# Attention with a quantised gate on one core: two rounds of four key tiles a step, and score banks lent to other fills

## The reference

```python
xn = layernorm(x)                                     # (4, 1024, 128)
Q, K, V = ((xn @ W).reshape(4, 1024, 16, 64) for W in (Wq, Wk, Wv))
raw = einsum('bshe,bthe->bsth', Q, K / sqrt(64))
attn = softmax(raw, axis=2)                           # over the 1024 keys t
A = gelu(einsum('bsth,bthe->bshe', attn, V).reshape(4, 1024, 1024))
s = xn + A @ Wpost
xq = quantise(xn), wq = quantise(weight)              # blocks of 32 onto a grid of 6-bit floats, times the block's scale
g = silu(xq @ wq.T + bias)
out = x + s * g
```

## Time and profile before

| | us |
|---|---|
| median of 3 runs | 1503.74 |
| lowest, highest | 1503.32, 1508.24 |
| profiled execution | 1504.28 |
| its span, first to last instruction | 1502.5 |
| TensorE busy | 1456.3 |
| GpSimd busy | 1144.7 |
| VectorE busy | 1080.7 |
| ScalarE busy | 804.7 |

### The profile page before, as it was taken

How to read it: one execution, slowest core, us unless ns; L and a number is a source line. 1 busy time by engine, 2 the same in 40 slices (tenths; PEclk the granted TensorE clock), 3 DMA queues, 4 the chain that set the end, 5 groups by cost and what they waited for, 6 DMA issues and landing times.

```text
span 1502.5 us, 25748 instructions
## 1 busy us (share of the span) xinstructions
PE 1456.3 (97%) x10369; PEld 794.2 (53%) x10369; DVE 1080.7 (72%) x1408; ACT 804.7 (54%) x1123; POOL 1144.7 (76%) x545
## 2 busy tenths in 40 slices
PE   5999999999999999999999999999999999999988
PEld 2555455555555555555555554555555555555478
DVE  6577777777777777777777777777777777777632
ACT  3455564555556565455555655555555555555563
POOL 0778788878887887887888778788778878877930
PEclk9999999999999999999999999999999999999999
DMA  2000000000000000000000000000000000002361
GB/s 76 1 8 15 8 15 29 16 8 15 15 8 15 15 13 24 15 14 8 15 15 15 8 15 14 9 15 15 8 15 8 1 1 1 1 1 80 118 220 49
DMA packets 25589, 35.40 MB, mean 24 GB/s; under 512 B 1792, under 2 KB 15872, under 8 KB 25472
## 3 DMA queue, kind: packets, MB, share of 16 engines
q1 hardware_dynamic: 25472, 33.76, 6.4%
HBM read 19.07 MB, written 14.68 MB: 22 GB/s over the span
## 4 chain that ended last, share of the span: by engine, by line
PE 88%; DVE 10%; issue 1%; ACT 1%; DMA 0%; POOL 0%; SPq 0%; ACTq 0%
PE acc L397 26%; PE scores L384 21%; PE peaks L368 11%; PE extra L287 8%; PE scores L388 7%; DVE half_maxes L807 5%; PE extra L317 4%; PE extra L300 4%; PE scores L456 4%; PE extra L324 2%; PE extra L338 1%; DVE extra L782 1%; DVE extra L783 1%; DVE extra L784 1%; DVE quant L785 1%
## 5 line engine op out<-in xcount | busy, mean ns | idle before, releaser
L696 POOL TENSOR_TENSOR prob_sum<-prob_sum,probs 128x1024 f32<-128x1024 f32 x384 | 912.1, 2375 | 236.7 <-ACT probs L571 209.3
L807 DVE TENSOR_REDUCE half_maxes<-peaks 128x2 f32<-128x1024 f32 x504 | 611.5, 1213 | 282.4 <-PE peaks L368 281.2
L571 ACT ACTIVATE probs<-scores 128x1024 f32<-128x1024 f32 x512 | 497.2, 1023 | 385.3 <-PE scores L388 375.4
L397 PE MATMUL acc<-probs,vals 128*64 128x512 f32 x2048 | 487.9, 597 | 0.0
L397 PEld LDWEIGHTS acc<-probs,vals 128*64 128x64 f32 x2048 | 137.2, 137 | 246.3 <-issue 218.1
L823 DVE RECIPROCAL inv_sum<-inv_sum 128x128 f32<-128x128 f32 x256 | 240.1, 941 | 0.0
L368 PE MATMUL peaks<-k_hi,q_hi 64*128 64x512 f32 x1008 | 226.0, 443 | 0.0
L384 PE MATMUL scores<-q_hi,k_hi 64*128 64x512 f32 x1024 | 202.7, 392 | 0.0
L388 PE MATMUL scores<-max_rows,ones_r 64*128 64x512 f32 x1024 | 202.2, 390 | 0.0
L384 PE MATMUL scores<-q_hi,k_lo 64*128 64x512 f32 x1024 | 202.1, 390 | 0.0
L384 PE MATMUL scores<-q_lo,k_hi 64*128 64x512 f32 x1024 | 202.0, 390 | 0.0
(11 more groups left out here) (147 smaller groups left out, 1025.6 us busy)
## 6 DMA issues: line engine op xcount, KB each, us to landing
att_scratch<-att SPq DMA_DIRECT2D x48, 256.0 KB, 2.0
probs<-att_scratch SPq DMA_DIRECT2D x8, 512.0 KB, 9.1
xTs<-att_scratch SPq DMA_DIRECT2D x4, 512.0 KB, 7.9
out_dram<-xn SPq DMA_DIRECT2D x8, 256.0 KB, 4.1
x_in<-in_L_attn_X SPq DMA_DIRECT2D x3, 512.0 KB, 4.0
q_hi_back<-att_scratch SPq DMA_DIRECT2D x2, 512.0 KB, 4.2
q_lo_back<-att_scratch SPq DMA_DIRECT2D x2, 512.0 KB, 5.0
k_hi_back<-att_scratch SPq DMA_DIRECT2D x2, 512.0 KB, 6.6
```

The lines of the kernel that those rows point to most:

```text
L397: last = mm(acc[own[h], :], vals[(s // 2) % 2][:, j, own[h]], probs[j][:, h, :], start=(j == 0), stop=(j == KT - 1), tile_position=col[h])
L571: sa.activation(probs[j][:, :, :], scores[j % 2][:, :, :], ACT.Exp, scale=DH ** -0.5).then_inc(probs_ready, 1)
L696: gp.tensor_tensor(prob_sum[s % 2][:, :, :], before[:, :, :], probs[j][:, :, :], ALU.add).then_inc(probs_summed, 1)
L807: v.tensor_reduce(half_maxes[:, :, f // 2, f % 2], peaks[:, :, :], AX.X, ALU.max).then_inc(peaks_read, 1)
```

## The change

A step now has two rounds of four key tiles. A round is: peak 0, two scores, peak 1, two scores, peaks 2 and 3, the fills "before", two value products, the lent fills, two value products, the fills "behind". In round 0 the value products are tiles 4 to 7 of the step before, in round 1 tiles 0 to 3 of this one.

- The fourth peak of a round (f = 3 and 7) goes into scores[0], behind the third exponential of the round; VectorE reduces it from there. The other three go through peaks.
- q, k, v, w and the later x fills leave extra: they go, two at a time, into the two banks of scores[1], amid the value products, behind the fourth exponential of the round. They have semaphores of their own, lent_filled and lent_read, and the next round's second score waits until they are read.
- VectorE: the join of the maxima stands right behind the last reduction, the spreading of the rows at the end of the round; the quantiser's two parts stand together in round 0 of the odd step; the inversion of den is split over two steps (parts 0 and 1 in round 1, parts 2 and 3 in round 0 of the next).
- ScalarE: four exponentials in a row, then the copies; the copy of the sums in round 0 of every step.
- GpSimd: only floor_blocks(0) stands earlier.

The diff, cut to its core:

```diff
     def extras(s, r):
         n, half = s // 2, s % 2
         before, behind = [], []
+        if r == 0:
+            if s > 0:
+                before.append(("den", s - 1))
+            if half == 1:
+                before.append(("quant", n))
+            elif n > 0:
+                behind.append(("turn_x", n - 1))
+        else:
+            if half == 0 and n > 0:
+                before.append(("ffn", n - 1))
+            if s + 1 < NS:
+                behind.append(("turn", s + 1))
+        return before, behind
+
+    def lent(s, r):
+        n, half = s // 2, s % 2
         if half == 0:
+            return [("qk"[r], n + 1, 0), ("qk"[r], n + 1, 1)] if n + 1 < NP else []
+        if r == 0:
+            return [("v", n + 1, 0), ("v", n + 1, 1)] if n + 1 < NP else []
+        if n == 0:
+            return [("w",)]
+        if n % HP == 4 and n // HP + 1 < B:
+            return [("x", n // HP + 1, 0), ("x", n // HP + 1, 1)]
+        return []
...
         def bank(use):
+            if use in lent_place:
+                return scores[1][:, lent_place[use], :]
             return first.get(use, extra[:, :])
...
-                above(pe, peaks_read, 8 * s + f)
+
+                place = scores[0] if f % 4 == 3 else peaks
+                if f % 4 == 3:
+                    pe.wait_ge(probs_ready, 8 * (s - 1) + f)
+                elif f % 4 == 0 and s > 1:
+                    pe.wait_ge(peaks_read, 8 * s + f - 1)
+                else:
+                    pe.wait_ge(peaks_read, 8 * s + f)
...
-                if j == 0 and s == 0:
-                    pe.wait_ge(peaks_read, 8)
+                if j == 0:
+                    pe.wait_ge(peaks_read, 8 * s + 8)
+                if j == 4 and s + 1 < NS:
+                    pe.wait_ge(peaks_read, 8 * s + 12)
+                if j % 4 == 1:
+                    above(pe, lent_read, lent_up_to[2 * s + j // 4])
...
             for s in range(NS):
-                for r in range(4):
+                for r in (0, 1):
                     before, behind = extras(s, r)
...
+                    peaks_here = (lambda f: peak(s + 1, 4 * r + f)) if s + 1 < NS else (lambda f: None)
+                    late = [(s, j) for j in range(4)] if r == 1 else [(s - 1, j) for j in range(4, 8)] if s > 0 else []
+                    peaks_here(0)
+                    score(s, 4 * r)
+                    score(s, 4 * r + 1)
+                    peaks_here(1)
+                    score(s, 4 * r + 2)
+                    score(s, 4 * r + 3)
+                    peaks_here(2)
+                    peaks_here(3)
                     for use in before:
                         run(use)
...
+                    for at in late[:2]:
+                        weigh(*at)
+                    if lent(s, r):
+                        pe.wait_ge(probs_ready, 8 * s + 4 * r + 4)
+                    for use in lent(s, r):
+                        run(use)
+                    for at in late[2:]:
+                        weigh(*at)
                     for use in behind:
                         run(use)
...
+                for r in (0, 1):
+                    for j in range(4 * r, 4 * r + 4):
+                        exps(s, j)
+                    if r == 0 and s > 0:
+                        copy_sums(s - 1)
+                    if r == 0 and half == 1:
                         unscale(n)
...
+                for r in (0, 1):
+                    for f in (4 * r, 4 * r + 1):
+                        if next_step:
+                            reduce_peaks(s + 1, f)
+                        if r == 0 and s > 1:
+                            invert(s - 2, 2 + f)
+                        if r == 1 and s > 0:
+                            invert(s - 1, f - 4)
                     if next_step:
...
+                        reduce_peaks(s + 1, 4 * r + 2)
+                        reduce_peaks(s + 1, 4 * r + 3)
+                    if r == 1 and next_step:
+                        join_maxima(s + 1)
+                    if r == 1 and half == 0 and n > 0:
+                        gate_argument(n - 1)
+                    if half == 0 and ahead:
+                        low(("qk"[r], n + 1, 0))
+                        low(("qk"[r], n + 1, 1))
+                    if half == 1 and r == 0:
+                        quantise_tile(n, 0)
+                        quantise_tile(n, 1)
```

More of the change, by code:

```diff
@@ L36, in extras @@
         before, behind = [], []
-        if half == 0:
[L38 to L59, removed]
+        if r == 0:
[13 more added lines that the diff above has]
+        n, half = s // 2, s % 2
+        if half == 0:
+            return [("qk"[r], n + 1, 0), ("qk"[r], n + 1, 1)] if n + 1 < NP else []
[6 more added lines that the diff above has]
+        return []
     FILLS = [("v", 0, 0), ("v", 0, 1), ("turn", 0)]
+    LENT = []
     for s in range(NS):
-        for r in range(4):
+        for r in (0, 1):
             for part in extras(s, r):
                 FILLS += part
+            LENT += lent(s, r)
     FILLS += [("den", NS - 1), ("turn_x", NP - 1), ("ffn", NP - 1)]
@@ L69, in gated_attention_kernel @@
     fill_number = {use: i for i, use in enumerate(u for u in FILLS if u[0] != "quant")}
+    lent_number = {use: i for i, use in enumerate(LENT)}
+    lent_place = {use: i for s in range(NS) for r in (0, 1) for i, use in enumerate(lent(s, r))}
+    lent_up_to = [0]
+    for s in range(NS):
+        for r in (0, 1):
+            lent_up_to.append(lent_up_to[-1] + len(lent(s, r)))
     own = [slice(0, DH), slice(DH, P)]
@@ L538, in copy_xT_later @@
                 is_filled(act, use)
-                sa.copy(xT[b][:, halves[half]], bank(use)).then_inc(extra_read, 1)
+                sa.copy(xT[b][:, halves[half]], bank(use)).then_inc(lent_read, 1)
             def high(use):
@@ L558, in copy_square @@
                 is_filled(act, use)
-                sa.copy(dst[:, :], extra[:, 0:P]).then_inc(extra_read, 1)
+                sa.copy(dst[:, :], bank(use)[:, 0:P]).then_inc(has_read(use), 1)
             def copy_acc(s):
@@ new lines, in _ @@
+                for r in (0, 1):
+                    for j in range(4 * r, 4 * r + 4):
[3 more added lines that the diff above has]
+                    if r == 0 and half == 1:
+                        unscale(n)
+                    if half == 0 and ahead:
+                        high(("qk"[r], n + 1, 0))
+                        high(("qk"[r], n + 1, 1))
+                    if half == 1 and r == 0 and ahead:
+                        copy_v(("v", n + 1, 0))
+                        copy_v(("v", n + 1, 1))
+                    if half == 1 and r == 1 and n == 0:
+                        copy_square(("w",), ffn_wT)
+                    if half == 1 and r == 1 and n % HP == 4 and later < B:
+                        copy_xT_later(("x", later, 0))
+                        copy_xT_later(("x", later, 1))
+                    if r == 0 and s > 0:
+                        copy_acc(s - 1)
+                    if r == 0 and half == 0 and n > 0:
+                        copy_square(("turn_x", n - 1), quant_T)
+                    if half == 0 and r == 1 and n % HP == 1 and n > 1:
@@ L631, in _ @@
                             root(part_of(later, 0))
[L632 to L633 removed]
+                        if half == 1 and r == 1 and n % HP == 3:
+                            scale_rows(later, 0)
+                        if half == 0 and r == 0 and n % HP == 4:
+                            scale_rows(later, 1)
             copy_acc(NS - 1)
@@ L910, in result @@
                 v.tensor_tensor(rows, rows, as_rows(x_back[c]), ALU.add).then_inc(result_done, 1)
-            for c in range(4):
+            for c in (2, 3):
                 invert(NS - 2, c)
```

120 lines of the change are left out of this document (33 added, 87 removed).

## The result

The changed kernel takes 1500.74 us in the median of 18 runs, the kernel before 1504.72 in 18 runs beside it: a ratio of 0.9973, with a 95% interval of 0.9965 to 0.998. It is 4 us faster where 11 us slower was forecast. The profiled execution took 1498.94 us with a span of 1497.1, which is 5.4 less than before.

What follows compares the result with a forecast made beforehand. TensorE, busy 97% of the span, was taken to bound the kernel. Span 1502.5 - 45.4 (crossings) - 26 (turned maxima) + 83 (four scores in a run) = 1514, so 1515 us forecast, range 1486 to 1530.

Steps and rivals of the forecast that it cites:

- Crossings: TensorE going between the 64*128 and 128*64 matmul forms and back: 128 fewer at 0.355 us each, -45.4 us.
- Turned maxima: TensorE's wait at the turn (L324) for VectorE's joined maxima would vanish: -26 us, ends -18.8 and -27.
- Fills lent: Projections, values and later inputs moved into scores[1] behind two value products: cover of 1.4 us each, no cost.
- Four scores in a run: Score banks reused too early, so TensorE waits and weight loads lie open: 0.65 us a round, +83 us (+35 to +97).
- the value of the shape: ScalarE's end to TensorE's next matmul taken as 0.14 us, from the row of the same 128x1024 shape.
- the prediction's own bound of 0.47 a round: Loss per round at the score-bank waits if release takes 0.06 us and the weight load stays in the open.
- The sum: Whole kernel: 1502.5 - 45.4 - 26 + 83 = 1514 us of span, 1515 us as the time.
- VectorE, ScalarE, GpSimd: Same work in less even order; VectorE's cover 1.0 us in an odd step's first round, ScalarE's copies no cost.
- rival B: GpSimd's sums come late for the denominators' matmul in odd steps, slower still: 1547 us; chance 0.09.
- rival C: TensorE's granted clock falls because of short idles: each 1% adds 15 us, 5% would make 1585; chance 0.03.
- rival A: Score-bank waits on TensorE are small, 0.27 to 0.50 us a round, and it is faster: 1467 to 1496; chance 0.29.
- D: No difference in kernel time: score-bank loss of 0.52 to 0.59 us a round, 1499 to 1508; chance 0.16.

Runs made afterwards that it cites:

- the kernel whose waits were up to 6.9 us long: The kernel before with VectorE's order evened out and the quantiser moved from the shared PSUM bank to SBUF: 1705.63 us.

## Why the prediction was wrong

- **Crossings, -45.4 us**: right, to some 2 us. The added crossing measured 0.34 us by the end times and 0.35 in its trace, 43 to 45 us for 128 of them.
- **Turned maxima, -26 us**: right. The wait is gone from the loop (18.8 us of idle time before, of which 1.6 stand ahead of the loop; 1.6 after), and the distances at the turn are 25.6 us shorter. The same wait taken out of the kernel before gave 23 by the medians and 25.7 by the traces.
- **Fills lent, no cost**: right. No matmul of a round in full swing waits for lent_read, and no lent fill is put down to a wait for probs but one, of 0.7 us.
- **Four scores in a run, +83 us**: this is the step that failed. The mechanism stands (the bank wanted too early at the third score and the fourth maxima fill, an open weight load of 0.105 behind each), but the term "TensorE's next matmul starts some time after ScalarE's end", taken as 0.14, is 0.05 here. In a usual round both waits are 0.09 shorter for it, 0.13 and 0.10 instead of 0.22 and 0.19; nine longer ones at the third score bring the means to 0.17 and 0.12. The 0.03 at the fourth score is 0. That makes 0.50 a round instead of 0.65, 63 us over 126 rounds instead of 83. The choice between the two kinds of rows was the error. I took the value of the shape, but two of the three rows released by that shape show 0.06 and 0.05, and the change of form, by which I explained two small ones away, doesn't hold for the last (1454.65). What tells the rows apart is whether a wait stands ahead of the awaited one. With 0.05 for both places the prediction's own bound of 0.47 a round gives 1493, and a sign of faster.
- **The sum**: -45.4 - 26 + 63 = -8 against -5.4 in the spans. The 3 us between are no more than the terms are known to: the crossings by the end times are 43 and not 45, and the shorter exponentials took 64.6 away and not 63. What the sum hides is that the merged rounds by themselves lose some 20 us (crossings and waits together), and that the freed turn of 25.6 us covers it.
- **VectorE, ScalarE, GpSimd**: right. The denominators (L342) wait for nothing; rival B didn't come. The granted clock was 1.00 in the loop; rival C didn't come either, at 43.7 to 44.0 us busy of 44. What the Trainium skill's page "TensorE: Matmul & The Clock Gate" tells in "A second HAM failure mode: psum-queue depth-cycling" doesn't show with these two idles a round, at a clock of 1.00; it was 0.92 in the loop of the kernel whose waits were up to 6.9 us long. (The 1.6 us that the prediction puts in the loop before stood ahead of it; the longest there was 1.33.)
- **Where the time fell**: rival A named the cause, a release of 0.06 us with the weight load in the open (0.47 a round), and had 0.29. The time itself lies in what I called D, no difference, 1499 to 1508: the nine longer waits cost 4 us more than A's 0.47 a round, and the sum missed by the 3 us above. Sum and break-even (0.56 a round) lay 0.09 apart, and one term was uncertain by 0.09 twice a round: with both signs inside one unmeasured term, the forecast of a sign deserved less than 0.55.

## What to carry to other kernels

Where a change trades a known cost for a tight reuse of a buffer, the reuse time is a sum of four terms, and the one from the releasing engine's end to the next matmul depends on how the wait is written: put the wait that will be late first, since a satisfied one written ahead of it cost 0.085 us each time. Price a crossing between tile forms (here 0.34 to 0.355 us) and a late engine in one queue before merging rounds: here the reordering of VectorE alone gave 23 us; the changed kernel, which has that gain in it too, gave 4, so merging the rounds itself lost some 20. A gain at the end can hide a part of the change that loses: try the parts one by one. And before moving a VectorE operand out of PSUM, see what GpSimd is doing.

## What the runs showed of the hardware that was not expected

- From an engine's end to the released weight load are 0.05 to 0.06 us when the awaited wait is the matmul's only or first one, and 0.11 (0.14 to the matmul) when a satisfied wait stands ahead of it; one behind it costs nothing (1521.97 and 1500.82 against 1500.74 us). The wait written second is an instruction of its own, of 0.051 us, ahead of the weight load.
- A weight load of 64x128 that stands behind a wait costs 0.105 us in the open (pairs of 0.338 instead of 0.231 us in the changed kernel's trace). The end times fit that it does so even where the wait is near zero: exponentials an eighth shorter took 25 us off, half as long 65.
- The quantiser's small VectorE operations went from 0.29 to as much as 2.4 us each when their operands moved from PSUM to SBUF beside a busy GpSimd; on SBUF with GpSimd idle they took 0.23 to 0.29.
